# An attention and feed-forward layer on eight cores: smaller accumulator banks, a second transpose bank, and weight copies moved from the start into the attention

## The reference

```python
h = layernorm(x)
Q, K, V = h*q_bind, h*k_bind, h*v_bind          # per head, q_bind = mean|bv| * sign(bv)
scores  = einsum(Q, K) / 32
attn    = where(causal, sigmoid(4*scores), 0)   # no softmax, so no row sums
x  = x + einsum(attn, V)
h2 = layernorm(x)
x  = x + h2 @ weight.T + bias + (h2 @ A.T) @ B.T
```

## Time and profile before

| | us |
|---|---|
| median of three runs | 11452.73 |
| lowest and highest | 11440.5, 11665.93 |
| the profiled execution | 11445.66 |
| its span on the slowest core (core 1) | 11444.1 |
| spans of the other cores | 11405.3 to 11434.7 |
| mean granted TensorE clock | 0.843 to 0.845 |

### The profile page before, as it was taken

The page is one execution under the profiler, slowest core; times in us unless marked ns, Lnnn a source line. Parts: engine busy times, 40 slices in busy tenths (PEclk is TensorE's granted clock), DMA queues, the critical chain, the costliest instruction groups (busy, mean ns, idle before and its releaser), DMA issues.

```text
span 11444.1 us, 101086 instructions; the slowest of 8 cores (11405.3 to 11444.1 us)
## 1 busy us (share of the span) xinstructions
PE 7311.6 (64%) x36337; PEld 3377.5 (30%) x36337; DVE 4468.2 (39%) x4897; ACT 1864.7 (16%) x2891; POOL 259.9 (2%) x494
## 2 busy tenths in 40 slices
PE   0046544554775766878677875787757778278478
PEld 0012221222332332333333332333323333133233
DVE  2355555554434343333433334334343434400300
ACT  0233423441210111111011111111101111100100
POOL 0000000000000000000000000000000000000000
PEclk9978877777887888989888987898878888589699
DMA  9554545454222222121222122212221221134233
GB/s 110 153 176 155 175 147 171 165 181 126 84 74 74 74 70 77 57 74 56 81 67 74 59 71 74 74 59 70 68 80 60 70 72 58 63 89 99 70 82 88
DMA packets 503783, 1065.22 MB, mean 93 GB/s; under 512 B 315829, under 2 KB 315845, under 8 KB 451013
## 3 DMA queue, kind: packets, MB, share of 16 engines
q1 hardware_dynamic: 445336, 672.85, 20.0%
q0 software_dynamic: 57952, 385.92, 11.6%
HBM read 974.72 MB, written 83.89 MB: 93 GB/s over the span
## 4 chain that ended last, share of the span: by engine, by line
PE 51%; DMA 24%; DVE 12%; issue 5%; ACT 4%; SPq 2%; another core or an unknown queue 1%; DVEq 1%; ACTq 0%; POOLq 0%; POOL 0%
PE pqk L516 19%; PE pav L561 19%; DMA khd<-xk 14%; PE py L860 8%; DMA kh<-xk 6%; DVE xb L485 3%; PE ptr L381 3%; DMA x1s<-ebuf 2%; SPq L84 2%; ACT sdump L334 2%; DVE QgT L438 1%; DVE attn L542 1%; DVE acc L578 1%; DMA kh<-xq 1%
## 5 line engine op out<-in xcount | busy, mean ns | idle before, releaser
L516 PE MATMUL pqk<-QgT,xbT 128*128 128x512 bf16 x12288 | 2847.8, 393 | 737.1 <-ACT stage L529 721.9
L561 PE MATMUL pav<-xb,attn 128*128 128x512 bf16 x12288 | 3033.2, 404 | 393.3 <-DVE attn L542 393.3
L529 ACT ACTIVATE stage<-pqk,cst 128x512 bf16<-128x512 f32 x1536 | 1055.8, 687 | 6567.4 <-DVE xbT L392 3804.5
L516 PEld LDWEIGHTS pqk<-QgT,xbT 128*128 128x128 bf16 x12288 | 1215.3, 100 | 2327.4 <-issue 1015.1
L561 PEld LDWEIGHTS pav<-xb,attn 128*128 128x128 bf16 x12288 | 1237.1, 103 | 1900.6 <-issue 776.2
L381 PE MATMUL ptr<-ident,xb 128*128 128x128 bf16 x6144 | 509.7, 231 | 1583.3 <-DVE xbT L392 1573.9
L542 DVE TENSOR_TENSOR attn<-stage,msk 128x1024 bf16<-128x1024 bf16 x768 | 941.0, 1225 | 1447.8 <-ACT stage L529 1433.4
L578 DVE SCALAR_TENSOR_TENSOR acc<-pav,acc 128x1024 f32<-128x1024 f32 x704 | 861.9, 1224 | 1235.4 <-PE pav L561 1189.0
L485 DVE TENSOR_SCALAR xb<-khd,mcache,rcache 128x1024 bf16<-128x1024 f32 x768 | 623.8, 812 | 1492.7 <-DMA khd<-xk 1471.3
L860 PE MATMUL py<-wtb,h2T 128*128 128x512 bf16 x4096 | 915.9, 382 | 224.3 <-DMA wtb<-wb 224.3
L381 PEld LDWEIGHTS ptr<-ident,xb 128*128 128x128 bf16 x6144 | 432.0, 103 | 1788.4 <-issue 1634.0
(11 more groups left out here) (110 smaller groups left out, 1395.0 us busy)
## 6 DMA issues: line engine op xcount, KB each, us to landing
khd<-xk SPq DMA_DIRECT2D x768, 512.0 KB, 4.8
kh<-xk POOLq DMA_DIRECT2D x256, 1024.0 KB, 5.6
msk<-mk SPq DMA_DIRECT2D x96, 1024.0 KB, 8.7
khd<-xq SPq DMA_DIRECT2D x128, 512.0 KB, 4.3
wb<-wgt POOLq DMA_DIRECT2D x4, 8192.0 KB, 202.2
kh<-xq POOLq DMA_DIRECT2D x32, 1024.0 KB, 6.0
y<-yb POOLq DMA_DIRECT2D x128, 256.0 KB, 2.4
x1s<-ebuf POOLq DMA_DIRECT2D x64, 256.0 KB, 4.6
```

Source lines behind the costliest of these rows:

```text
L516: E.matmul(pqk[bank][:], xbT[b][:, HD * dc + 128 * sc:HD * dc + 128 * (sc + 1)], QgT[:, CH * dc + 512 * th:CH * dc + 512 * (th + 1)], star ...
L529: E.activation(out=stage[ss][:, 512 * th:512 * (th + 1)], in_=pqk[bank][:], func=AF.Sigmoid, scale=cst[:, 0:1]))
L561: E.matmul(pav[bank][:, 512 * dh:512 * (dh + 1)], attn[:, CH * sc + 128 * tc:CH * sc + 128 * (tc + 1)], xb[b][:, HD * sc + 512 * dh:HD * s ...
```

## The change

It has three parts.

1. The four DMAs of `wb` at the start go. Instead 16 DMAs of 256 rows each stand among the statistics' tasks, two behind each of the groups of key blocks 1 to 8, on the same queue of POOL.
2. The PSUM banks are shared out anew: four `pqk` instead of three, two `ptr` instead of one, and two `pav` of 512 columns (one bank each) instead of 1024.
3. `plan_av` evicts each half (dh) of a row piece by itself, so there are 16 groups of 8 matmuls with 16 evictions of 128x512 instead of 8 of 128x1024. A transposition is still called behind every 16 matmuls.

```diff
-            wb_done = None
-            for i in range(4):
-                wb_done = dma("gp", wb_d[i * 1024:(i + 1) * 1024, :],
-                              wgt_d[i * 1024:(i + 1) * 1024, :])
...
             pqk = [AT.enter_context(nc.psum_tensor(f"pqk{i}", [128, 512], F32))
-                   for i in range(3)]
-            pav = [AT.enter_context(nc.psum_tensor(f"pav{i}", [128, 1024], F32))
+                   for i in range(4)]
+            pav = [AT.enter_context(nc.psum_tensor(f"pav{i}", [128, 512], F32))
                    for i in range(2)]
-            ptr = [AT.enter_context(nc.psum_tensor("ptr0", [128, 1024], BF16))]
+            ptr = [AT.enter_context(nc.psum_tensor(f"ptr{i}", [128, 1024], BF16))
+                   for i in range(2)]
...
             def plan_xpose(xb_buf, xbT_buf, st, av):
-                ps = 0
+                ps = state["tr"] % 2
+                state["tr"] += 1
...
                     for th in range(2):
-                        bank = gi % 3
+                        bank = gi % 4
...
             def plan_av(q, h, k, ttv, xtasks):
                 b = k % 2
                 W("t", "V", ttv)
+                gj = 0
                 for tc in range(NS):
-                    bank = tc % 2
-                    av_bank[bank].acquire("t")
-                    avv = None
                     for dh in range(2):
+                        bank = gj % 2
+                        av_bank[bank].acquire("t")
+                        avv = None
                         for sc in range(NS):
...
-                    av_bank[bank].release([("V", sv)])
-                    if xtasks:
-                        xtasks.pop(0)()
+                        av_bank[bank].release([("V", sv)])
+                        gj += 1
+                        if gj % 2 == 0 and xtasks:
+                            xtasks.pop(0)()
...
+            def _wb_task(i):
+                def t():
+                    dma("gp", wb_d[i * 256:(i + 1) * 256, :],
+                        wgt_d[i * 256:(i + 1) * 256, :])
+                return t
...
                 stat_tasks.append(_fin_task(kind, idx, box))
                 stat_group_end[(kind, idx)] = len(stat_tasks)
+                if kind == "kv" and 1 <= idx <= 8 and wbp < 16:
+                    stat_tasks.append(_wb_task(wbp))
+                    stat_tasks.append(_wb_task(wbp + 1))
+                    wbp += 2
+                    stat_group_end[(kind, idx)] = len(stat_tasks)
...
+            while stat_tasks:
+                stat_tasks.popleft()()
+            wb_done = ("GP", cnt["GP"])
```

More of the change, by code:

```diff
@@ L312, in build_program @@
             xbT_slot = [Slot(), Slot()]
-            ptr_slot = [Slot()]
+            ptr_slot = [Slot(), Slot()]
             stage_slot = [Slot(), Slot()]
@@ L316, in build_program @@
             msk_slot = Slot()
-            qk_bank = [Slot() for _ in range(3)]
+            qk_bank = [Slot() for _ in range(4)]
             av_bank = [Slot() for _ in range(2)]
@@ L561, in plan_av @@
                                    E.matmul(
-                                       pav[bank][:, 512 * dh:512 * (dh + 1)],
+                                       pav[bank][:],
                                        attn[:, CH * sc + 128 * tc:CH * sc + 128 * (tc + 1)],
@@ L565, in plan_av @@
                                        start=(sc == 0), stop=(sc == NS - 1)))
-                            if dh == 1 and sc == NS - 1:
+                            if sc == NS - 1:
                                 avv = op("t", "T", bf_)
@@ L569, in plan_av @@
                                 opq("t", bf_)
[L570 to L580, removed]
-                    av_bank[bank].release([("V", sv)])
-                    if xtasks:
-                        xtasks.pop(0)()
+                        state["av_last"] = avv
+                        W("v", "T", avv)
+                        dst = acc[:, CH * tc + 512 * dh:CH * tc + 512 * (dh + 1)]
+                        if k == 0:
+                            sv = op("v", "V", lambda E, d=dst, bank=bank:
+                                    E.tensor_copy(d, pav[bank][:]))
+                        else:
+                            sv = op("v", "V", lambda E, d=dst, bank=bank:
+                                    E.scalar_tensor_tensor(
+                                        out=d, in0=pav[bank][:], scalar=1.0, in1=d,
+                                        op0=OP.mult, op1=OP.add))
+                        av_bank[bank].release([("V", sv)])
+                        gj += 1
+                        if gj % 2 == 0 and xtasks:
+                            xtasks.pop(0)()
                 while xtasks:
@@ L647, in build_program @@
             plan_stats_group("kv", 0)
+            def _wb_task(i):
[3 more added lines that the diff above has]
+                return t
             stat_group_end = {}
+            wbp = 0
             for kind, idx in ([("kv", k) for k in range(1, 8)] + [("q", 1)]
```

## The result

| | us |
|---|---|
| changed kernel, runs compared | 11621.8 to 11633.8 (four), 11767.7 (a fifth) |
| kernel before, runs compared | 11437.2 to 11472.1 (five) |
| ratio | 1.0181, 95% interval 1.0124 to 1.0238 |
| forecast | 11650 against 11445.7, a ratio of 1.018 |

The kernel became slower, and the interval leaves no doubt that it did. How much hangs on the fifth run: with it the ratio is 1.018, that of the forecast to the third digit; the other four, which lie within 12 us, have a mean of 11630 us against 11450.5 before, a ratio of 1.016 and 180 us. In the profiled execution of the changed kernel cores 4 to 7 ran disturbed, so its numbers here are those of cores 0 to 3, and its rows those of core 1. Their median span is 11610 us, 189 us above the 11421 us of the same cores before.

The account below looks back on a forecast made before the run. It took the AV phase as bound by DVE's eight normalisations, which wait for `khd`, and then PE's remaining work; 11445.7 - 195 + 219 + 202 - 7 - 13 = 11651.7, rounded to 11650 us, range 11520 to 11770.

Parts of the forecast that it names:

- part 1b: Attention visits 0 to 6 and 8: copy pairs delay the third `khd`, 26.5 us each (33 in visit 8), +219 us.
- How the numbers follow: Closing odds on the whole kernel's time: 0.65 within 2%, 0.28 slower, 0.07 faster; 2% taken as the limit of no change.
- Part 1a: Prologue: without the weight copies four short loads and `bl` no longer wait behind them, -195 us.
- The bound of -184: Prologue: smallest gain from removing the copies, with 4.5 us taken for the short loads; the other bound was -207.
- keep their pace, less a microsecond: Visits with a pair: the five loads behind the third `khd` follow at their usual spacing, less a microsecond.
- hidden: Visits with a pair: `kh` loads behind it are needed only some 50 us later, in the next QK phase, so cost nothing.
- nothing move: QK phases: claimed to show no change in the profile after.
- visit 8: Where the eighth pair falls: third `khd` used at 1875.5 instead of 1841.77, +33 us.
- The rule of whole packets: DMA queues: an engine drains a whole packet of some 9 to 17 descriptors from one ring before turning to the next.
- the first rival: Attention: `khd` loads pass the copies in one packet's turn, 144 us instead of 219, 11575 us in all; chance 0.2.
- Part 2: AV phase: 16 matmuls move behind the stall, +3.46 us, earlier resumption gives back 1.33; +2.13 per visit, +202 us over 95.
- Part 3: Banks elsewhere: first preparation -7 us once; sweeps' ends -13 us together, including 1.73 us in each of five places.

Follow-up runs that it names:

- e1_copies: Kernel before with only the weight copies moved, in pairs behind groups 1 to 8 of the statistics' tasks, banks and evictions unchanged; 11457 us beside 11421 to 11428.
- e10_single: Kernel before with seven copies of 256 rows placed singly behind groups 1 to 7 and the other nine in QK phases; 11329 us beside 11425.
- e3_small: Changed kernel with each copy of 256 rows split into two DMAs of 2048 columns, packets writing 4 KB instead of 32; ratio 1.025 to the kernel before.
- e8_banks_inter: Kernel before with the new banks and half evictions, and six of eight normalisations each moved behind an eviction; copies at the start; ratio 0.8434.

## Why the prediction was right, and where it was not

The time was right, and the two main mechanisms with it; what failed is the step from the time to a direction, and inside part 1b a pair of steps whose errors offset each other.

- **The step that failed** is the last, in "How the numbers follow". The terms added up to 1.7 to 1.8% slower, and the prediction then set that against "about 2% from no change", put 0.65 on within 2% and 0.28 on slower. No row bore out those 2%. What the runs showed in their place: four runs of the changed kernel lie within 12 us and five of the kernel before within 35 us, the loss is 180 us, and the ratio's interval, 1.2 to 2.4% slower, does not contain "no change". None of the terms by stage was off by more than 17 us, so the sum was clear of noise, and the text should have said that the kernel becomes slower, by a little less than 2%.
- **Part 1a** held: -197 us to the first QK phase against -202. In e1_copies, which has the old `ptr`, it is -194 against -195. The four loads that had waited behind the copies now take 2.4 and 3.2 us (`rowX`), 4.1 and 5.1 us (`al`), where I had taken 2.5 and 3.5. It was the mechanism as told: short loads wait for the copies' packets. (The bound of -184 counts `bl` at 4.5 us as well; the four loads alone give -189.)
- **Part 1b** held in its sum, and there the closeness is in part luck. Seven pairs cost (209.6 - 8 x 2.1)/7 = 27.5 us each, and 26.5 in e1_copies, against 26.5. In e1_copies, over visits 0 to 6 and four cores, a pair lasts 34.1 us and not 38, and the third normalisation is 21.5 us late, so 12.6 us of the pair do lie ahead of it, as the prediction had it. But the loads behind the third don't "keep their pace, less a microsecond", and the `kh` loads behind the pair are not "hidden": the eighth normalisation is 24.4 us late, and the visit 26.5 us longer. Nor does "nothing move" in the QK phases: those of visits 1 to 7, with their products, take 81.0 us instead of 79.0. The pair was priced 4 us too high, and what follows it, at one microsecond, 4 us too low. With a single copy of 17.3 us the third is 8.8 us late, the eighth 10.3 us, and the visit 12.9 us longer, so half a pair costs half and not the 6 us that an overlap of fixed length would leave.
- What the visits grow by follows how long the copies' packets hold each engine: 12.9 us of 16.2 in e10_single, 26.5 of 31.2 in e1_copies, 27.5 of 31.9 in the changed kernel, (1299.8 - 1070.9 - 16.8)/7 = 30.3 of 35.0 in e3_small. That is 80 to 87% each time. No run tells why just this much stays hidden.
- For visit 8 I had 33 us, and the eighth normalisation came 27.4 us late. The copies ran faster there than in the prologue, which is below.
- **The rule of whole packets**, the first rival, is out for these loads: 45 packets against 42 in the window from 505 us. It would not have mattered much for the sum: in e3_small the third normalisation of visit 0 came 19 us sooner and nothing was won.
- **Part 2** held: +2.0 us per steady visit against +2.13, resumed 0.84 us after the eviction as computed. e8_banks_inter shows that it has the cause that was given: without the stall the new banks cost nothing.
- **Part 3** was too small: 2.1 to 3.0 us at the sweeps' ends instead of 1.73. What PE has to do behind its wait there shrank by 1.6 to 1.7 us, as computed; the rest is that the wait ends 0.4 to 1.3 us sooner, counted from the start of the QK phase, and why it does stays open. In the first preparation the second `ptr` gave 3 us (418.1 against 421.4 in e1_copies), where I had 7, which is no more than the cores differ by.

What the prediction didn't ask is what the stall itself is worth. It named the eight normalisations in DVE's list as what the phase is bound by, and then priced only how the banks shift the edge of that stall.

## What to carry to other kernels

When an engine's in-order list puts all preparations of the next step ahead of the releases of this one, more or other buffers only move the edge of the stall: here they made 1.4% more or 1.2% less, and the order of the list 15.7%. Interleave the list first, and count the buffers afterwards. A copy in the background cost 80 to 87% of the time that it held the DMA engines where loads were awaited, with large packets and with small; put it where the trace shows the engines idle, not where the queue happens to be free. And when the terms of a forecast add up to more than the runs scatter, forecast the direction that they give.

## What the runs showed of the hardware

**Two queues on the same DMA engines went packet for packet**, though one had 32 KB packets and the other 64 bytes or 4 KB (visit 0 above). The load with the small packets pays: a `khd` of 512 KB, asked for while a pair of copies ran, held its normalisation up by 30.42 us instead of 4.96.

**The copies' packets became faster as the cores drifted apart.** At the start all eight cores copy at once. Of the 434 packets of the earlier trace rows, 16 are closing ones of four bytes (13.70 MB are 418 packets of 32 KB), so a packet takes 0.976 x 128 us x 16 / 418 = 4.8 us of an engine, and not the 4.72 of the prediction. In the changed kernel the cores reach the last mask product of visit 0 between 485 and 497 us, and that of visit 6 between 1422 and 1482 us. The queue of copies on core 1, from 486 to 500 us and from 1425 to 1440 us:

```profile
q0 software_dynamic: 59, 1.74, 103.6%
```
```profile
q0 software_dynamic: 88, 2.36, 105.9%
```

Without the closing packets, 6 and 16 of them, the first is 1.036 x 14 x 16 / 53 = 4.4 us per packet, the second 1.059 x 15 x 16 / 72 = 3.5 us. On core 1 the span of the whole pair falls from 37 to 28 us.

The other runs fit. The starts of the copies on the eight cores, first and last of them, and the mean span of what was copied:

| | apart, visit 0 | span | apart, visit 6 | span |
|---|---|---|---|---|
| changed kernel, pair | 12 us | 38.8 us | 60 us | 31.2 us |
| e1_copies, pair | 13 us | 38.0 us | 39 us | 28.9 us |
| e3_small, pair in 4 KB packets | 15 us | 47.3 us | 26 us | 47.3 us |
| e10_single, one copy | 12 us | 17.4 us | 19 us | 17.8 us |

Where the cores stay together, the copies don't become faster. This suggests that the cores share what the copies need; no run here held the cores apart on purpose.
